# Splitting each step of a running maximum into two halves of the feature axis on VectorE (edge convolution, one core)

## The reference, cut to what matters

```python
h = relu(layernorm(x))
x_i, x_j = h[dst], h[src]
msg = concat([x_i, x_j - x_i]) @ W.T + b
out = x + segment_max(msg, dst)
```

## Time and profile before

| | |
|---|---|
| median of 3 runs | 993.31 us (989.05 to 994.56) |
| span of the profiled execution | 993.8 us |
| DVE busy | 846.5 us, 85% |
| POOL busy | 713.8 us, 72% |
| PE busy | 564.1 us, 57% |
| L1134, the chain's steps | 527, 185.6 us busy, 352 ns each |

### The profile page before, as it was taken

One profiled execution on the slowest core, in us unless ns is written; L12 is line 12 of the kernel. 1 busy time (PEld: TensorE's weight loads), 2 busy tenths in 40 slices (PEclk: granted clock), 3 DMA queues, 4 the chain that ended last, 5 costly groups with the idle time before them and its releaser, 6 DMA issues.

```text
span 993.8 us, 7917 instructions
## 1 busy us (share of the span) xinstructions
PE 564.1 (57%) x2393; PEld 265.1 (27%) x2393; DVE 846.5 (85%) x1237; ACT 577.9 (58%) x255; POOL 713.8 (72%) x644
## 2 busy tenths in 40 slices
PE   2556970000002366766776676788878888676560
PEld 2443640000001122322222232333333333222240
DVE  7899899987785598999989999899999999758573
ACT  3775113000038999597996987496797976844000
POOL 1587878888875677677767676676777677777745
PEclk9898995555555779888878987999999999988875
DMA  8831222212146466656657776998988778754344
GB/s 256 194 97 21 70 71 79 67 50 77 55 145 217 142 208 223 197 174 222 179 170 232 255 253 201 295 296 300 338 302 321 278 239 259 227 186 139 73 79 148
DMA packets 62901, 182.11 MB, mean 183 GB/s; under 512 B 20358, under 2 KB 33140, under 8 KB 56315
## 3 DMA queue, kind: packets, MB, share of 16 engines
q1 hardware_dynamic: 42530, 140.13, 40.7%
q0 software_dynamic: 20144, 40.52, 17.1%
q10 hardware_dynamic: 184, 0.96, 0.3%
HBM read 127.34 MB, written 55.04 MB: 184 GB/s over the span
## 4 chain that ended last, share of the span: by engine, by line
POOL 29%; DVE 26%; issue 19%; DMA 13%; PE 8%; ACT 3%; POOLq 0%; DVEq 0%; SPq 0%; PEldq 0%
POOL rows L669 22%; DVE acc L1191 10%; DMA rows<-near_table,idx 8%; PE ps L787 8%; DVE maxima L1134 5%; POOL ohs L641 4%; POOL hT L648 3%; DVE hT L1141 3%; DMA running_max<-maxima 2%; DVE pos L878 2%; DVE hT L1154 1%; DVE ohs L1179 1%; DMA ohs<-in_dst,begin_i 1%; DMA ohs<-winners 1%; DVE hT L1146 1%
## 5 line engine op out<-in xcount | busy, mean ns | idle before, releaser
L669 POOL DMA_INDIRECT rows<-near_table,idx x527 | 600.3, 1139 | 206.0 <-issue 138.8
L787 PE MATMUL ps<-ohs,near 128*128 128x481 bf16 x1443 | 351.9, 401 | 142.6 <-DVE acc L1191 119.7
L1191 DVE TENSOR_TENSOR acc<-ps,acc 128x1924 f32<-128x1924 f32 x192 | 336.5, 1779 | 21.8 <-PE ps L787 21.6
L1134 DVE SCALAR_TENSOR_TENSOR maxima<-maxima,fresh,rows 128x128 f32<-128x128 f32 x527 | 185.6, 352 | 72.6 <-DMA rows<-near_table,idx 56.2
L787 PEld LDWEIGHTS ps<-ohs,near 128*128 128x128 bf16 x1443 | 143.7, 105 | 350.1 <-DVE acc L1191 125.8
L548 ACT ACTIVATE ohs<-ohs,neg_l 128x6272 bf16<-128x6272 bf16 x25 | 137.9, 5518 | 123.4 <-DMA ohs<-winners 123.4
L541 ACT ACTIVATE hT<-k,off 128x2400 bf16<-128x2400 int16 x49 | 108.9, 2281 | 131.7 <-DVE hT L1146 115.6
L550 ACT ACTIVATE ohs<-ohs 128x6272 bf16<-128x6272 bf16 x25 | 135.8, 5431 | 0.8
L787 PE MATMUL ps<-sorts_mem,near 128*128 128x481 bf16 x468 | 107.8, 385 | 32.7 <-DVE acc L1191 28.6
L773 PE MATMUL ps<-flags,ones 128*128 128x8 f32 x2 | 0.6, 356 | 173.0 <-DVE spare L1167 173.0
L641 POOL DMA_INDIRECT ohs<-src_pad,start_i x49 | 55.0, 1122 | 34.9 <-DVE start_i L891 20.5
(11 more groups left out here) (173 smaller groups left out, 517.4 us busy)
## 6 DMA issues: line engine op xcount, KB each, us to landing
ohs<-winners SPq DMA_DIRECT2D x37, 1568.0 KB, 7.7
running_max<-maxima SPq DMA_DIRECT2D x90, 512.0 KB, 5.1
sorts_mem<-winners SPq DMA_DIRECT2D x12, 1568.0 KB, 8.0
rows<-near_table,idx POOLq DMA_INDIRECT x527
acc<-in_x SPq DMA_DIRECT2D x6, 512.0 KB, 8.2
near_table<-acc SPq DMA_DIRECT2D x12, 256.0 KB, 4.5
base<-in_x SPq DMA_DIRECT2D x1, 2744.0 KB
out_x<-hT SPq DMA_DIRECT2D x12, 224.0 KB
```

Of the source, the lines that this page charges most:

```text
L669: nc.gpsimd.indirect_dma_start(rows[:, n % (SLOTS * GATHERS), :], None, near_table[:, :], bass.IndirectOffsetOnAxis(idx[:, n:n + 1], 0)).t ...
L787: last = nc.tensor.matmul(bank(4 * (n % 2) + c - UNITS[r][0])[:, 0:CHUNK], near[:, t, part, :], oh[t % OHS][:, at:at + CHUNK], start=part ...
L1134: V.scalar_tensor_tensor(run_at(n + 1), run_at(n), fresh[:, n:n + 1], rows[:, n % (SLOTS * GATHERS), :], ALU.add, ALU.max).then_inc(chain, 1)
L1191: V.tensor_tensor(into, found, into, ALU.max).then_inc(max_done, 1)
```

## The change

Each step of the chain is made as two instructions, one for features 0 to 63 and one for features 64 to 127. Each half waits only for the same half of the step before, so that two chains run in turn on DVE. `chain` then counts halves, and the counts that SP and POOL wait for are doubled. No other work, buffer or order changes.

```diff
             def maxima_store(i):
-                sp.wait_ge(chain, (i + 1) * STEPS - (i == all_blocks - 1))
+                sp.wait_ge(chain, 2 * ((i + 1) * STEPS - (i == all_blocks - 1)))
...
                 if b >= SLOTS:
-                    pool.wait_ge(chain, (b - SLOTS + 1) * GATHERS)
+                    pool.wait_ge(chain, 2 * (b - SLOTS + 1) * GATHERS)
...
-                if n and is_step(n):
-                    dve.wait_ge(chain, n)
                 if i and n % STEPS == STEPS - 1 and n < all_steps - 1:
                     dve.wait_ge(maxima_out[(i - 1) % 2], 16 * stores_until(i - 1))
                 if is_step(n):
-                    V.scalar_tensor_tensor(run_at(n + 1), run_at(n), fresh[:, n:n + 1],
-                                           rows[:, n % (SLOTS * GATHERS), :], ALU.add, ALU.max).then_inc(chain, 1)
+                    for half in range(2):
+                        at = slice(half * D // 2, (half + 1) * D // 2)
+                        if n:
+
+                            dve.wait_ge(chain, 2 * n - 1 + half)
+                        V.scalar_tensor_tensor(run_at(n + 1)[:, at], run_at(n)[:, at], fresh[:, n:n + 1],
+                                               rows[:, n % (SLOTS * GATHERS), at], ALU.add, ALU.max).then_inc(chain, 1)
```

## The result

The changed kernel takes 1006.43 us (median of 4 runs, 1004.88 to 1008.12) against 993.09 (4 runs, 989.05 to 994.56). The profiled execution took 1005.26 us with a span of 1003.6, so 9.8 us more than the span before. The other 3.5 us come from which execution was profiled: in every run on record the time is 1.6 to 1.7 us longer than the span. The runs of each kernel differ among themselves by 3 to 5.5 us.

What follows compares the result with a forecast made beforehand. DVE was taken to bound the kernel from 331 to 620 us, POOL after. 31 batches x 0.14 = 4.3 us, plus 0.3 for two more batches, gave 997.9 from the 993.3 median; forecast 998, range 993 to 1005.

Steps and rivals of the forecast that it cites:

- Extra time of the chain's steps vanishes there into these waits: Before 331 us: DVE's 25.2 us of waits for gathers absorb the longer batches, so nothing was counted there.
- The cost of a batch: On DVE, per batch of four steps made as eight halves: 0.14 us more, upper bound 0.20.
- Rivals 3 and 4: Halves on DVE: more overlap gives a gain, 987 us, 6%; no overlap gives 1028 to 1060 us, 3%.
- The count of batches: From 331 to 620 us: 31 of the 45 batches lie on the path, costing 4.3 us.
- Rival 5: From 331 to 620 us: PE's clock falls to 0.80, adding 4 us to its products, 1002 us; 7%.
- rival 6: From 331 to 620 us: more is absorbed, 15 batches count, 2 us, 995 us; 12%.
- Behind 620 us: POOL and its transfers hold back DVE; the extra 0.14 us per batch falls on DVE alone and is covered.
- DVE's final wait for gathers: Behind 850 us: DVE's 30.6 us of waits take up the extra time and shrink by some 5 us.
- The ring: Gather slots: POOL's lead over begun steps; 20 means DVE limits POOL, expected still at 615 to 625 us.
- rival 2: DVE bounds the kernel up to 850 us: 47 to 88 batches count, 6.6 to 12.4 us, 1000 to 1006; 15%.

Runs made afterwards that it cites:

- joint halves: Halves only for steps 0 to 111, both halves waiting for the whole step before, against the kernel before: 998.42 us against 996.34.
- plain time: Whole steps as in the kernel before, one to three independent DVE instructions added behind each of the first 28 batches: 997.1, 1090.27 (before there 1088.95), 995.96, 994.77 us.
- the kernel with three additions: Kernel before, whole steps, with three independent 26-column DVE instructions added behind each of the first 28 batches: 994.77 us against 996.34.
- early halves alone: Halves only for steps 0 to 111, whole steps after, against the kernel before: 1005.63 us against 990.19, one run each, on a chip like the result's.
- late halves: Whole steps for 0 to 111, halves from step 112 on, against the kernel before on slower chips: ratios 1.0107, 1.0146 and 1.018.
- mid ones: Halves only for steps 112 to 291, whole before and after, against the kernel before on a slower chip: 1095.94 us, ratio 1.0048.

## Why the prediction was wrong

- **The step that failed** is "Extra time of the chain's steps vanishes there into these waits", of the stage before 331 us. It cost 9.2 us instead of 0, two thirds of the result's 13.3. The row behind it was right (DVE does wait there for 25.2 us), and joint halves show that the wait can take up 10.0 of 14.6 us. What I missed is that the waits were in good part made by DVE's own work: POOL's gathers are held up by DVE's list-making, and the chain of waits had POOL's L669 at 52% of that stage. Behind alternating halves 3 of 5 gathers are held through two TENSOR_SCALARs where none was before, and the gathers of the stage take 8.8 us longer. A gather's duration there, 177.59 / 125 = 1.42 us against 0.94 alone, was in the trace and I didn't ask for its reason. Even plain time did not quite vanish: of 28 times 0.10, 0.15, 0.20 and 0.28 us the stage kept 1.8, 1.1, 3.5 and 5.8 us, 26 to 74% (the second against the 222.7 us of its kind of chip).
- **The cost of a batch** was right: +0.15 us (0.14 forecast), halves 0.196 us apart, 276 ns each, no idle between. Rivals 3 and 4 (apart by 0.13 or by 0.315 us) are excluded by it. L836's row was the nearest and gave the right figure.
- **The count of batches** was right in size. Batches 28 to 68 lose 4.7 us, 4.7 / 0.15 = 31 batches; 31 x 0.14 = 4.3 us was the forecast. That it fits to the batch is partly luck: the same stretch takes 252.8 to 255.6 us in five other kernels with whole steps there, on chips like this one. Rival 5 (clock) is excluded by the 0.85, and the 4.7 speaks against rival 6 (more absorbed).
- **Behind 620 us** the place was half right. DVE's final wait for gathers shrank, by 12.0 us and not 5. The ring stands at 20 up to 818 us, so DVE stays the limit longer, as in rival 2; yet its price is absent, for the stretch behind batch 68 is 3.6 us shorter. The halves don't make it so: the kernel with three additions, whose steps are whole, has the same 362.8 there, and the one with early halves alone has 366.3. Rival 2's upper 1006 us comes near the measured 1006.43 by luck. On the slower chips late halves do cost 1.1 to 1.8% and mid ones 0.5%, which suggests, with intervals that overlap, that batches behind 73 count there, as rival 2 had it. Late halves alone were not run on a chip like that of the result; what they cost there is open.
- **The missing rival** was a loss in the stage that I had written off. None of the six had a price there, so the range had none either.

## What to carry to other kernels

A wait is cover only if the thing waited for doesn't depend on the waiting engine's own work: where POOL's gathers take longer beside some DVE instructions than alone (here 1.42 us on average against 0.94), the two engines set each other's time. There a change that adds 0.15 us to a batch can cost a single gather 1.5 us, and the same eight halves can cost more when they take less of DVE's time (stage 232.4 us against 226.7 for joint halves). Before a stage is written off in a forecast, compare the duration of the gathers there with the shortest anywhere, and look in order of time for what lengthens them. Splitting a small DVE instruction pays the fixed part twice (0.196 us per 64 columns against 0.355 per 128 of a dependent step). On one chip, with one run each, sharing out whole steps between other pieces took 10.2 us less than before, where two chains cost 13.3 in the result.

## What the runs showed of the hardware

- A gather (indirect transfer of 128 rows) on POOL takes 0.94 us alone. One that begins inside a DVE instruction of the list-making (int32 TENSOR_SCALAR and COPY_PREDICATED of some 2400 columns, TENSOR_TENSOR) ends some 0.8 us behind it (15 of 19 and 31 of 33 in the kernel before), and one that begins inside a chain step with at least 0.13 us of it left can do so too (up to 1.07 us).
- Caught by a TENSOR_SCALAR that begins after it, a gather ends 0.11 to 0.14 us behind that one. With two TENSOR_SCALARs in a row it can be held through both, 3.25 us instead of 1.75 (22 of 25 behind alternating halves, none of 55 behind whole steps). COPY_PREDICATED that begins after it doesn't catch it.
- Two halves with their waits already met start 0.196 us apart at 64 columns, the same as L836's instructions at 128 columns.
- One kernel took 993 us on some chips and 1089 on others, with the first 28 batches alike (223.2 and 222.7 us).
